# A two-layer transformer kernel in eight batches: ten sliding maxima in the dense stage, the third layer two linear units into the pairs stage, the third slide weighing at the dense stage's head

## What is computed

```python
def reference(x, ...):                       # 8 x 512 x 128
    xn = layernorm(x)
    x = x + L0_attn(xn) + L0_ffn(xn)
    xn = layernorm(x)
    return x + L1_attn(xn) + L1_ffn(xn)

def L0_attn(x):
    h = rmsnorm(x, norm_w)
    q, k, v = h @ Wq, h @ Wk, h @ Wv         # 16 heads of 8
    lin = linear attention, causal, of taylor_feature_map(q @ Wqf), (k @ Wkf)
    win = softmax(q k^T / sqrt(8)) over keys t-64..t, times v
    return x + concat(lin, win) @ Wout

def L0_ffn(x):                               # ternary weights, hidden 512
    h = silu(x w1^T * s1) * (x w2^T * s2)
    h = gelu(h h1^T * s)                     # 512 x 512
    h = gelu(h h2^T * s)                     # 512 x 512
    return h w3^T * s3                       # the "third layer"

def L1_attn(x):                              # layernorm with gamma, beta; 16 heads
    return causal_softmax_attention(...) @ Wo + bo

def L1_ffn(x):                               # top 2 of 8 experts
    gates = softmax over top_k(x @ Wg^T, 2)
    return sum over e of gates_e * (gelu(x W1_e + b1) @ W2_e + b2)
```

## Time and profile before

| | us |
|---|---|
| median of three runs | 1280.85 (1279.3 to 1280.9) |
| profiled execution | 1279.02 |
| its span in the trace | 1277.3 |
| mean granted clock of PE | 0.974 |
| PE busy | 1152.3 (90%) |
| DVE busy | 865.0 (68%) |
| ACT busy | 743.6 (58%) |
| POOL busy | 649.1 (51%) |
| chain that ended last, by engine | PE 52%, DVE 21%, ACT 13%, issue 7% |

### The profile page before, as it was taken

How to read it: one execution, slowest core, us unless ns; L and a number is a source line. 1 busy time by engine, 2 the same in 40 slices (tenths; PEclk the granted TensorE clock), 3 DMA queues, 4 the chain that set the end, 5 groups by cost and what they waited for, 6 DMA issues and landing times.

```text
span 1277.3 us, 26679 instructions
## 1 busy us (share of the span) xinstructions
PE 1152.3 (90%) x9122; PEld 743.5 (58%) x9122; DVE 865.0 (68%) x3433; ACT 743.6 (58%) x1580; POOL 649.1 (51%) x846
## 2 busy tenths in 40 slices
PE   5988999998999899989998999899989867988997
PEld 2445754574457545754575457544754556874896
DVE  4066588658865886588558865886588656874563
ACT  2356357735773577457745774567546624557675
POOL 4475254535444544454444544454445435685577
PEclk9999999999999999999999999999999978999999
DMA  7601620162015301540154015401571016541233
GB/s 237 156 3 47 186 72 14 55 184 75 13 56 160 99 14 52 139 121 15 43 150 120 15 40 151 119 17 40 152 224 44 2 26 147 83 68 27 44 55 40
DMA packets 123961, 105.53 MB, mean 83 GB/s; under 512 B 15242, under 2 KB 118578, under 8 KB 123826
## 3 DMA queue, kind: packets, MB, share of 16 engines
q1 hardware_dynamic: 102162, 85.89, 24.6%
q0 software_dynamic: 13792, 9.54, 5.2%
q10 hardware_dynamic: 7872, 8.39, 1.9%
HBM read 58.59 MB, written 46.37 MB: 82 GB/s over the span
## 4 chain that ended last, share of the span: by engine, by line
PE 52%; DVE 21%; ACT 13%; issue 7%; POOL 5%; DMA 2%; DVEq 0%; SPq 0%; POOLq 0%; ACTq 0%
PE bank L701 12%; PE heads L766 12%; ACT probs L1118 8%; PE bank L680 7%; PE bank L708 7%; DVE hT_s L1586 4%; DVE xnT_s L1586 4%; DVE hrow L1586 3%; PE bank L1051 2%; PE bank L676 2%; PE bank L691 2%; PE bank L1059 2%; POOL out L1363 2%; DVE spare L1586 2%; PE bank L816 2%
## 5 line engine op out<-in xcount | busy, mean ns | idle before, releaser
L1118 ACT ACTIVATE probs<-bank 128x512 f32<-128x512 f32 (+2 forms) x896 | 442.0, 584 | 210.3 <-PE bank L708 204.5
L1310 POOL TENSOR_SCALAR_AFFINE_SELECT probs<-probs 128x384 f32<-128x384 f32 x256 | 127.2, 518 | 236.5 <-ACT probs L1118 233.6
L766 PE MATMUL heads<-probs,V 128*18 128x192 f32 (+9 forms) x3072 | 196.3, 396 | 10.6 <-POOL probs L1313 4.6
L708 PE MATMUL bank<-K,Q 128*128 128x192 bf16 (+4 forms) x1024 | 199.7, 273 | 4.6 <-DVE mx_s L1586 1.2
L708 PE MATMUL bank<-Q,K 128*128 128x192 bf16 (+4 forms) x1024 | 174.3, 274 | 16.9 <-ACT probs L1118 7.0
L1363 POOL DMA_INDIRECT out<-h1T_s x78 | 123.7, 1586 | 60.1 <-ACT h1T_s L1271 39.9
L766 PEld LDWEIGHTS heads<-probs,V 128*9 128x9 f32 (+1 forms) x3072 | 78.7, 94 | 123.3 <-issue 85.8
L708 PE MATMUL bank<-QM,K 128*128 128x512 bf16 (+3 forms) x512 | 123.8, 307 | 24.8 <-DVE mx_s L1586 17.9
L1263 ACT ACTIVATE h2T_s<-bank,h1T_s 128x128 f32<-128x128 f32 x312 | 88.9, 368 | 93.6 <-PE bank L1051 82.3
L708 PEld LDWEIGHTS bank<-Q,K 128*128 128x128 bf16 x1024 | 81.0, 98 | 88.1 <-ACT probs L1118 31.2
L708 PEld LDWEIGHTS bank<-K,Q 128*128 128x128 bf16 x1024 | 86.5, 99 | 64.5 <-DVE mx_c L1586 14.3
(11 more groups left out here) (241 smaller groups left out, 2216.8 us busy)
## 6 DMA issues: line engine op xcount, KB each, us to landing
K<-slots_of_k SPq DMA_DIRECT2D x64, 256.0 KB, 4.3
Q<-slots_of_q SPq DMA_DIRECT2D x15, 1024.0 KB, 10.1
QM<-slots_of_qm SPq DMA_DIRECT2D x8, 1024.0 KB, 9.3
h1T_s<-sorted_rows SPq DMA_DIRECT2D x78, 65.0 KB
slots_of_q<-Q SPq DMA_DIRECT2D x8, 384.0 KB, 2.6
slots_of_k<-QM SPq DMA_DIRECT2D x8, 384.0 KB, 2.9
slots_of_qm<-Q SPq DMA_DIRECT2D x8, 384.0 KB, 2.6
slots_of_k<-Q SPq DMA_DIRECT2D x8, 384.0 KB
```

Source lines behind the costliest of these rows:

```text
L708: mm = pe.matmul(to[:, at:at + right.shape[1]], left, right, start=True, stop=True, skip_group_check=True)
L766: mm = pe.matmul(heads[ROWS * i:ROWS * i + n, P * j:P * j + widths[j]], V[:, j, g // 2, i, first:first + n], slot_of(kind, 2 * g + i // 2) ...
L1118: return act.activation(to, bank, func, scale=scale, bias=bias).then_inc(taken_sem(run, unit), 1)
L1310: pool.affine_select(out=three, in_=three, compare_op=ALU.is_ge, fill=0.0, base=0, pattern=[[0, 3], [1, P]], channel_multiplier=-1)
```

## The change

- `EARLY = 10` of the 32 sliding maxima are computed in the dense stage of the batch before, two each behind `h1_2`, `h1_3`, `cols`, `h2_0` and `h2_1` (table `EARLY_AT`). PE waits for `slots_k1` and `slots_q1`, the fetches of K's lower half and Q, ahead of the first of them; DVE writes their masked bank back to PSUM in place (`in_place`). In the opening part all ten follow `h2_3`.
- The third layer stands behind two linear units, ahead of all maxima of its stage, where it stood behind five and eight maxima. `AHEAD` is 8 for 12, `LEAD` 10 for 8, and `scores_by` is a new function.
- The weighing of the third group of sliding heads, `weigh(now, SLIDE, 2)`, stands at the head of the dense stage, where it stood behind `h1_0`.
- `h2_2` is whole ahead of `hT2`, and `BEGUN = 4` products of `h2_3` stand ahead of `k2`; before, nine and three of `h2_2` stood there and `h2_3` was whole behind `v2`.
- `copy_heads(now, SLIDE, 1)` moves from DVE to ACT. ACT's gelu of `h2_2` moves ahead of the split of k2. DVE takes `v1` later. `first_stats` is issued at causal unit 24, not 31; POOL's `power(nxt, 1)` at pair 6, not 7.
- POOL splits q1 and k1 behind mask pair 3 and qm1 behind pair 4, where it did so behind all eight pairs. SP loads x ahead of the mid and low sends and stores y behind them; it sends q1's and k1's parts ahead of qm1's, and fetches QM, then waits for the last sliding unit, then K's lower half, Q, K's upper half.
- The setup products take the bank of `SETUP_BANK`.

```diff
+BEGUN = 4
-AHEAD, LEAD = 12, 8
+EARLY, AHEAD, LEAD = 10, 8, 10

 def maxima(before):
-    sliding = [("smax", n) for n in range(len(SMAX_UNITS))]
+    sliding = [("smax", n) for n in range(EARLY, len(SMAX_UNITS))]
     return sliding[:AHEAD] + [("cmax", n) for n in range(PAIRS)] + sliding[AHEAD:] if before else sliding
...
 def scores_by(before, d):
     if not before:
-        return 8 + (PAIRS - 8) * d // (len(SMAX_UNITS) - 1)
-    return LEAD * d // AHEAD if d < AHEAD else LEAD + 61 * (d + 1 - AHEAD) // 60
+        return 8 + (PAIRS - 8) * d // (len(SMAX_UNITS) - EARLY - 1)
+    if d < AHEAD:
+        return 2 + (LEAD - 2) * d // AHEAD
+    return min(LEAD + (PAIRS + HALF - LEAD) * (d - AHEAD) // (SCORED - AHEAD), 2 * PAIRS)

 def third_at(before):
-    return 8 if before else 0
+    return 0
...
+EARLY_AT = {"h1_1": (0, 0), "h1_2": (0, 2), "h1_3": (2, 4), "cols": (4, 6), "h2_0": (6, 8), "h2_1": (8, 10), "h2_2": (10, 10)}
...
                 if after:
-                    for n in (1, 2):
-                        for name in ("q1", "k1", "qm1"):
-                            send((b, 1), name, n)
+                    for name, n in (("q1", 1), ("k1", 1), ("q1", 2), ("k1", 2), ("qm1", 1), ("qm1", 2)):
+                        send((b, 1), name, n)
+                if before and this:
+                    store(run, b - 1)
...
                 if after:
+                    sp.wait_ge(S["sent_k1"], due("sent_k1", (b, 1), SENT))
+                    fetch_sent((b, 1), "qm1")
                     if this:
                         sp.wait_ge(taken_sem(run, SLIDE_UNITS[-1]), taken_at(run, SLIDE_UNITS[-1]))
...
-                    sp.wait_ge(S["sent_k1"], due("sent_k1", (b, 1), SENT))
                     fetch("k1", LOWER)
-                    fetch_sent((b, 1), "qm1")
+                    fetch_sent((b, 1), "q1")
                     fetch("k1", UPPER, "upper")
-                    fetch_sent((b, 1), "q1")
...
             def dense_stage(run, after):
...
+                weigh(now, SLIDE, 2)
                 if after:
...
-                weigh(now, SLIDE, 2)
-                if after:
                     dense_low(run, "h1_1", layer1, 1)
+                    early(run, "h1_1")
                 weigh(now, SLIDE, 3)
                 if after:
                     dense_low(run, "h1_2", layer1, 2)
+                    early(run, "h1_2")
                 turn_heads(run, now, SLIDE, 1)
...
                     dense_low(run, "h2_1", layer2, 1)
-                    dense_low(run, "h2_2", layer2, 2, range(9))
+                    early(run, "h2_1")
+                    dense_low(run, "h2_2", layer2, 2)
...
-                    dense_low(run, "h2_2", layer2, 2, range(9, 3 * FC))
+                    dense_low(run, "h2_3", layer2, 3, range(BEGUN))
+                    early(run, "h2_2")
                 wait_taken(run, "hT2")
...
-                    dense_low(run, "h2_3", layer2, 3)
+                    dense_low(run, "h2_3", layer2, 3, range(BEGUN, 3 * FC))
...
-                if after:
-                    split_rest(nxt, ("q1", "k1", "qm1"))
+                    if p == 3 and after:
+                        split_rest(nxt, ("q1", "k1"))
+                    if p == 4 and after:
+                        split_rest(nxt, ("qm1",))
```

100 lines of the change are left out of this document (70 added, 30 removed).

## The result

The changed kernel takes 1299.9 us in the median of four runs (1295.66 to 1306.82), against 1280.16 for the kernel before: 1.0153 times as long, with a 95% interval of 1.0135 to 1.0172. The forecast was 1286 with a range of 1266 to 1298, so the direction was right and the size was not. Its profiled execution took 1300.72 us, with a span of 1299.0. Two executions of later runs are left out of all that follows, one of e8_split3_back (1293.73 us, at a lower granted clock than its others) and one of e11_power7 (2195.96 us); what slowed them isn't known.

A forecast was written before the change was run, and what follows sets the result against it. PE was taken to bound the kernel, working 121.88 of 129.7 us a batch. Terms of 3.6 - 1.85 + 0.8 - 0.55 - 1.15 - 0.25 gave +0.6 a batch, +4.2 for seven, plus 2.5 for the first: about 1286 us, range 1266 to 1298.

The forecast's parts named there:

- A: Dense stage up to q2's product: claimed +3.6 us a batch.
- ten early units and four products of h2_3: Dense stage: sliding maxima and products moved ahead of q2 add +1.5 and +0.95 us a batch.
- wait at the head: First weighing of the dense stage: PE waits 1.1 to 1.4 us for POOL's masks, not 0.59; +0.5.
- wait for Q1: First early maximum in the dense stage: PE waits for Q1's fetch, +1.3 us a batch, from 0 to 4.
- wait for `hrow` ahead of hT2: Dense stage: this wait goes because h2_2 is now whole ahead of it, -0.65 us a batch.
- slow clock within the stage: Dense stage: no term given, so 0; half clock was priced only in the later causal scores.
- Q1 in time: Rival: Q1's fetch lands without a wait at the early maxima; 1276.6 us, or 1271 if the clock holds; chance 0.38.
- From q2 to the causal maximum: Stretch from q2's end to DVE's first causal maximum: -1.85 us a batch, with q2's fetch limiting the gain.
- Clock behind it: Causal scores behind PE's idle stretch after the third layer run at half clock: +0.8 us a batch, 0 to 1.6.
- rest of the pairs stage: Pairs stage: ACT's lead over DVE -0.55, shorter end section -1.15, earlier `power` -0.25 us a batch.
- The first batch: Opening part: ten maxima run with nothing beside them ahead of the third layer, +2.5 us once, 0 to 4.
- The wait for Q1 is long: Rival: PE stands 2.1 to 4.1 us a batch at the early maxima, slow clock following; 1291 to 1304 us; chance 0.12.

The follow-up runs named there:

- e8_split3_back: The changed kernel with qm1's split moved behind mask pair 3 and the third slide weighing put back behind h1_0; 1280.07 us.
- e11_power7: The changed kernel with qm1's split moved behind mask pair 3 and POOL's `power` back at causal pair 7; 1284.64 us.
- e1: The changed kernel with the third slide weighing put back behind h1_0; 1291.28 us.
- e9: The kernel before with only POOL's splits moved, q1 and k1 behind mask pair 3 and qm1 behind pair 4; 1286.8 us.
- e7: The changed kernel with only qm1's split moved, behind mask pair 3 with q1 and k1; 1279.09 us.
- e4: The changed kernel with SP fetching Q1 ahead of QM, the weighing staying at the head; 1293.21 us.
- the best combination: The changed kernel with six early maxima, twelve ahead of the causal ones, qm1's split behind pair 3 and the weighing behind h1_0; 1272.89 us.

## Why the prediction was wrong, point by point

The step that failed is the sum for the dense stage, A: +3.6 us a batch forecast, 5.93 measured. Its terms, in us a batch, from the waits and timelines of the two profiled executions:

| term of A | forecast | measured |
|---|---|---|
| ten early units and four products of h2_3 | +1.5 + 0.95 | +2.4 (PE's busy time in batch 2, which has no slow stretch) |
| wait at the head | +0.5 | +1.08 |
| wait for Q1 | +1.3 | +0.86 |
| wait for `hrow` ahead of hT2 | -0.65 | +0.37 |
| slow clock within the stage | 0 | about +1.2 (what is left) |
| sum | +3.6 | +5.93 |

- **The slow clock, at nothing**, is the largest miss. I priced its fall behind the long idle before the causal maxima, and not behind the idle that I had just computed at the head, nor behind the wait for Q1, for which only the rival had it. It costs about 1.55 us each time, in five of the six steady batches, three at the head and two behind the wait for Q1, and about twice that in batch 0, which had half of it before the change.
- **The wait for hrow2** was misread. The 3.9 us of the earlier trace rows aren't in the dense stage: five of the six waits stand 7 us behind the turning, in the slide stage, for the first norm's `hrow`, and the sixth in the opening. Ahead of hT2 PE didn't wait at all. Batch 4 of the kernel before, in the slide stage and ahead of hT2, then the changed kernel ahead of hT2:

```profile
616.46 0.66 PE L676 MATMUL bank<-ident_s,hrow 128*128 128x128 f32 x4 [0.69 <-DVE hrow L1537]
668.19 0.66 PE L676 MATMUL bank<-ident_s,hrow 128*128 128x128 f32 x4
```

```profile
684.84 0.66 PE L703 MATMUL bank<-ident_s,hrow 128*128 128x128 f32 x4 [0.37 <-DVE hrow L1586]
```

So there was nothing to save, and a wait came instead; it is in every kernel with ten early maxima and in none with six. The saving of 0.65 was a term without a source, 1.0 us a batch in all.

- **The wait at the head**: the mechanism was named, mask pair 5 behind the split of qm1, and its bound of 1.1 held. It was sized at 1.1 to 1.4 us of wait in place of 0.59; measured are 1.64. One reason is that POOL and DVE slow each other: I took the cast and the subtraction at 1.09 and 1.17, where they took 1.06 and 1.48. I also looked for no effect on DVE, whose instructions beside the split took 0.4 and 0.8 us more and made a second wait of 1.35 (e1, e9) behind the first, so that moving the weighing back doesn't undo the loss. The Trainium skill's "SBUF — State Buffer" (SBUF: two separate sides) says of the port pair that GpSimd and VectorE share that it is held for a whole instruction, and that a VectorE instruction with two SBUF inputs needs it against a GpSimd instruction that reads SBUF. The trace agrees as far as durations show it: 0.68 and 0.69 us became 1.09 and 1.46 beside the split, and the same 0.69 came back in e7. I used such a rule only for a lower bound of POOL's price, at 0, and not for DVE's side.
- **The Q1 wait**, +1.3. Its landing was right: forecast 14.9 us behind the end of the slide work, measured 13.0 to 16.7, in the mean 15.2. PE came late instead, slowed by the head, and waited in three of seven batches, 6.0 us together, 0.86 each. The bounds held. The fit from the Trainium skill's "DMA: Bandwidth & Descriptors" (Anatomy of one DMA), by which the prediction had Q1 in time, is given there for DMAs that GpSimd issues; SP issues these.
- **From q2 to the causal maximum**, -1.85: measured -2.25, with the fetch as the bound, as forecast: its wait is 20.9 us in seven. The idle stretch of 3.7 us was 3.0.
- **Clock behind it**, +0.8, and the **rest of the pairs stage**, -1.95: together -1.15 forecast, and -1.62 with +0.42 in the slide stretch measured, -1.2. The third layer takes 3.79 us, as forecast; the section at the end is 4.0 us in batch 4, not under it. `power` had the wrong sign at its own place: its wait at the causal weighing went from 0.26 to 0.70. But its move also took away the wait for `hrow` in the slide stage (0.73), and with it undone in e11 the slide stretch is as long. So it doesn't explain the +0.42. A wait of 0.3 for ACT where the heads are turned is new there, in seven batches 2.2 us against 0.7; the rest stays open.
- **The first batch**, +2.5: the third layer started at 66.12 in place of 60.34, 5.8 us later, of which 3.6 were left at the end of that pairs stage. An early unit takes DVE 0.58 us in the mean, where other sliding units take 0.52; the reading of the accumulator behind it takes 0.14 us in place of 0.08.

So the sum for a batch was +0.6 and is +2.5: the dense stage is 2.3 us over its forecast (5.9 for 3.6), the rest 0.4 under. Two sums of the prediction don't come out of their terms. With the waits at the head and for Q1 at 0, A is 1.8 us less, not 0.3; and the long wait of 4.1 us gives 1305, and 1317 with the slow clock, not 1304. "The wait for Q1 is long" was the rival with this time (1291 to 1304). What it describes, over 2 us of wait with the slow clock behind it, is in batches 5 and 6; but e4, without any wait for Q1, gets back some 5 of 19.7 us only. Most of the loss has the same form at the head of the stage, some 12 us earlier, and from another cause. I gave the rival 0.12 and let the range end at 1298, inside it.

## What to carry to other kernels

When work is moved to an earlier place on an engine, look for that engine's gap and not for its order: in the changed kernel the same split costs 20 us behind mask pair 4, where the slide work ends, and nothing behind pair 3, where POOL stood idle for 5 us. Price its neighbours too: what is moved on POOL changes DVE's durations, and PE may then wait for DVE. Where a profile shows the clock fall behind an idle stretch, every new wait of PE in the sum needs that fall as a second term, with a chance. Look up where a wait stands in time before you count on its going: a list of waits by releaser joins places that have nothing to do with each other. And test the parts of a change one by one: the third layer alone gave as much as the best combination, within the noise.

## What the runs showed of the hardware

- POOL's cast and subtraction beside DVE's two-operand instructions: DVE 0.68 to 1.09 us and 0.69 to 1.46, POOL's subtraction 1.16 to 1.48, its cast 0.61 to 1.06, the same within 0.01 us in two kernels.
- The granted clock fell to 0.50 behind PE waits as short as 0.6 to 1.7 us at the head of the dense stage, in 5, 14 and 22 of 30, 30 and 36 batches by the length of the wait, and each time cost about 1.55 us. Single executions of such kernels lie further apart: those of e8 between 1274.41 and 1287.44, those of the kernel before beside them between 1277.83 and 1281.69. That the slow stretches make the difference isn't shown, as one execution of each kernel was profiled.
- A fetch of 1 MB that is issued within 2 us of 1.5 MB ahead of it landed 9.4 to 13.1 us later (Q1 of seven batches, mean 11.5; 11.4 was forecast).
